# Features of the last head group weighed and decayed on VectorE, and the first set's indirect writes ended one step sooner

## The reference, cut to what matters

```
qs = softmax(q) ; ks = softmax(k)             # over the 128 features of a head
gl = log_sigmoid(k) / 16
S  = S * exp(gl) + ks x v ; o_gla = qs . S    # gated linear attention, along the tokens
y  = softmax(rot(q) rot(k)^T / sqrt(128)) v   # ordinary causal attention
o  = 0.5 * y + 0.5 * o_gla ; out = o @ Wo
```

## Time and profile before

| | before |
|---|---|
| time, median of 3 runs | 944.18 us (944.08 to 945.03) |
| profiled execution: time, span | 935.75 us, 933.5 us |
| mean granted TensorE clock | 0.994 |
| PE busy | 895.2 us (96%) |
| DVE busy | 679.4 us (73%) |
| ACT busy | 663.2 us (71%) |
| POOL busy | 635.4 us (68%) |
| chain that ended last | PE 77%, DVE 9%, ACT 5%, POOL 4%, issue 3% |

### The profile page before, as it was taken

The page is one execution under the profiler, slowest core; times in us unless marked ns, Lnnn a source line. Parts: engine busy times, 40 slices in busy tenths (PEclk is TensorE's granted clock), DMA queues, the critical chain, the costliest instruction groups (busy, mean ns, idle before and its releaser), DMA issues.

```text
span 933.5 us, 18329 instructions
## 1 busy us (share of the span) xinstructions
PE 895.2 (96%) x5145; PEld 706.8 (76%) x5145; DVE 679.4 (73%) x2010; ACT 663.2 (71%) x2147; POOL 635.4 (68%) x603
## 2 busy tenths in 40 slices
PE   7899999999999999999999999999999989799996
PEld 4577878777777777778788878787776766598885
DVE  5877877676767676767676978877888967475457
ACT  6687777777777777777686877778767767354656
POOL 6967676767566666768676767877656898546441
PEclk9999999999999999999999999999999999999999
DMA  7100100000000000620000001000003111125355
GB/s 266 35 12 29 29 24 1 6 13 7 1 0 0 0 0 7 178 62 1 1 1 2 1 1 44 1 1 17 17 17 106 40 61 41 57 86 148 109 149 202
DMA packets 30969, 41.46 MB, mean 44 GB/s; under 512 B 3230, under 2 KB 25631, under 8 KB 30624
## 3 DMA queue, kind: packets, MB, share of 16 engines
q1 hardware_dynamic: 27472, 31.98, 11.4%
q0 software_dynamic: 3408, 8.43, 2.5%
HBM read 24.72 MB, written 16.59 MB: 44 GB/s over the span
## 4 chain that ended last, share of the span: by engine, by line
PE 77%; DVE 9%; ACT 5%; POOL 4%; issue 3%; DMA 1%; DVEq 0%; POOLq 0%; ACTq 0%
PE PR L518 12%; PE OA L631 12%; PE S L585 10%; PE MS L604 8%; PE S L613 7%; PE OA L593 5%; PE OA L624 4%; PE S L731 3%; PE OA L748 3%; PE PR L564 3%; PE PR L558 3%; POOL slot_x L1717 1%; ACT eqk L879 1%; PE MS L547 1%; DVE pr L1111 1%
## 5 line engine op out<-in xcount | busy, mean ns | idle before, releaser
L1644 POOL TENSOR_TENSOR qd<-eqk,eg 128x512 f32<-128x512 f32 x63 | 75.0, 1190 | 132.3 <-issue 127.6
L631 PE MATMUL OA<-wT,V 128*128 128x512 f32 x320 | 148.4, 594 | 0.0
L841 ACT ACTIVATE S<-S,nm 128x128 f32<-128x128 f32 (+3 forms) x256 | 126.4, 494 | 6.6 <-DVE nm L1077 5.8
L1077 DVE CUSTOM_DVE_ANT_0 S<-S,maskb 128x128 f32<-128x128 f32 (+3 forms) x256 | 118.2, 518 | 13.0 <-PE S L585 11.8
L879 ACT ACTIVATE eqk<-qkv,nmx 128x128 f32<-128x128 f32 x320 | 124.3, 396 | 4.5 <-DVE nmx L1152 4.4
L1632 POOL TENSOR_TENSOR eqk<-eqk,rse 128x640 f32<-128x640 f32 x63 | 79.5, 1263 | 60.1 <-DVE rse L1195 37.0
L631 PEld LDWEIGHTS OA<-wT,V 128*128 128x128 f32 x320 | 59.8, 191 | 69.7 <-issue 69.7
L1111 DVE TENSOR_TENSOR pr<-S,rl 128x256 f32<-128x256 f32 (+3 forms) x128 | 105.5, 825 | 4.5
L1621 POOL TENSOR_TENSOR rp<-qkv,cos 128x640 f32<-128x640 f32 x64 | 99.5, 1555 | 6.8 <-ACT qkv L869 5.8
L1624 POOL TENSOR_TENSOR rp<-rp,rt 128x640 f32<-128x640 f32 x64 | 99.4, 1553 | 5.0
L1621 POOL TENSOR_TENSOR rt<-qkv,sin 128x640 f32<-128x640 f32 x64 | 99.4, 1552 | 0.0
(11 more groups left out here) (259 smaller groups left out, 2443.4 us busy)
## 6 DMA issues: line engine op xcount, KB each, us to landing
qkv<-slot_x SPq DMA_DIRECT2D x39, 129.0 KB, 2.1
slot_x<-zero SPq DMA_DIRECT2D x3, 1290.0 KB, 15.3
stage<-in_wgu SPq DMA_DIRECT2D x8, 352.0 KB, 3.1
stage<-in_wqkv SPq DMA_DIRECT2D x6, 384.0 KB, 3.7
xraw<-in_x_cols SPq DMA_DIRECT2D x16, 128.0 KB, 2.4
acc<-in_x_rows SPq DMA_DIRECT2D x1, 2048.0 KB, 11.1
dn_w<-in_wdn SPq DMA_DIRECT2D x1, 2048.0 KB, 8.2
pr<-plane SPq DMA_DIRECT2D x8, 256.0 KB, 3.9
```

Of the source, the lines that this page charges most:

```text
L631: last = pe.matmul(OA[:, :], V[:, j, :], wT[:, j, :], start=(c == 0 and j == 0), stop=(j == c))
L841: nc.scalar.activation(S[:, h, 0:n], S[:, h, 0:n], ACT.Exp, bias=nm[:, h:h + 1], scale=-1.0, accum_out=ls[:, h:h + 1]).then_inc(s_exp, 1)
L1077: nc.vector.tensor_tensor_reduce(out=S[:, h, 0:n], in0=S[:, h, 0:n], in1=maskb[:, N - n:N], scale=-1.0, scalar=FAR, op0=ALU.add, op1=ALU.m ...
```

## The change

Decay and weighing of chunks 60 to 63 (all of group 15) go from POOL to DVE. They are issued at steps 27 to 30, on DVE between the second half of the normalisation and `mask_gla`. The 24 writes of the first set stand at steps 25 to 30 with 4 in each step, where before step 30 had 6, step 31 had 2 and step 28 had none.

```
-        SEND_AT = {25: (0, 2), 26: (2, 4), 27: (4, 6), 29: (6, 8), 30: (8, 11), 31: (11, 12)}
+        SEND_AT = {25: (0, 2), 26: (2, 4), 27: (4, 6), 28: (6, 8), 29: (8, 10), 30: (10, 12)}
...
                 normalise(g, c, 1)
+                if isinstance(g, int) and C * (NG - 1) <= C * g + c + 1 < NU:
+                    decay(g, c + 1)
                 mask_gla(g, c)
...
                 later(pool, s_o, C * g + c)
-                if not (last and c == 3):
+                here = not isinstance(g, int) or C * g + c + 1 < C * (NG - 1)
+                if here:
                     weigh_features(g, c + 1)
                 move_v(g, c)
-                if not (last and c == 3):
+                if here:
                     decay(g, c + 1)
```

## The result

The changed kernel takes 947.89 us, the median of 9 runs (947.08 to 949.65), and the kernel before 944.58 us beside it (9 runs, 943.49 to 946.32). The ratio is 1.0033, with a 95% interval of 1.0023 to 1.0042: 3.3 us slower by the medians. The forecast was 944.5, and the range ended at 947.3.

The account below looks back on a forecast made before the run. PE, busy 96% of the span, was taken as the bound. Terms -6.1 - 2.4 + 3.1 + 4.8 + 0.3 + 0.65 = +0.35 gave 936.1 us profiled, and 8.43 carried over gave 944.5; range 936.3 to 947.3.

Parts of the forecast that it names:

- the clock in step 27: Step 27: PE's wait of 2.6 us was expected to cost no clock, so nothing was charged.
- rival C: Gaps in step 27 lower PE's clock: 1.7 us more, 946.2 us, up to 947.6 if step 29's slack fails; chance 0.21.
- The clock in step 29: Step 29: a slow clock after PE's 4.2 us wait, mostly absorbed by slack; term +0.3, bounds 0 and 1.7.
- PE's slack of 1.4 us: Step 29: PE's scores are ready before DVE uses them, expected to absorb about 1.4 of 1.7 us of slow clock.
- The blocking: Steps 27 and 29: DVE's decay and POOL's rotation block each other in turns; terms +3.1 and +4.8.
- The bounds: Limits on blocking: no blocking 0 in step 27, +0.4 in step 29; one wait +0.4 and +1.7.
- rival B: Partial blocking: one wait at each place gives 938.4 us, one of two places free 940 to 941.5; chance 0.15.
- rival A: No blocking in steps 27 and 29, POOL waits for DVE's five instructions: -7.45, 936.7 us; chance 0.15.
- Steps 28, 30 and 31: Step 28: decay wait gone, -2.4; step 30: later addition to `acc`, +0.65; step 31: page wait and slow clock gone, -6.1.
- it cannot be more than the wait: Step 28: the gain from removing PE's wait for the decay, -2.4, was capped at that wait's length.
- The last write: POOL's last write was expected near 791, with 6 us spare, so PE's page wait in step 31 goes.
- The level: The timed median was expected to lie 8.43 us over the profiled time, as before (944.18 against 935.75).

Follow-up runs that it names:

- after_again: The changed kernel, unedited, timed and profiled a second time: 937.95 us against 936.81 for the kernel before, ratio 1.0018.
- before_again: The kernel before, unedited, timed and profiled once more: 936.62 us against 936.51 beside it.
- decay_only: The changed kernel with the old table of writes, so only the decay moved to DVE: 937.9 us, 1.002 of the kernel before.
- sends_only: The kernel before with only the new table of writes, decay still on POOL: 932.28 us, 0.9957 of the kernel before.
- warm_gap: The changed kernel with products of zeros on PE in the gaps of steps 27 and 29: 933.79 us, 0.9972 of the kernel before.
- after_third: The changed kernel, unedited, timed and profiled a third time: 943.58 us, 0.9997 of the kernel before.
- hold_rotation: The changed kernel with POOL's rotation held until DVE's decay is through, steps 27 to 29: 928.94 us, 0.9922 of the kernel before.
- psum_operand: The changed kernel with the last group's decay on DVE reading one operand from PSUM instead of SBUF: 928.32 us, 0.9907 of the kernel before.
- after: The first measurement and profile of the changed kernel: 947.89 us against 944.58 for the kernel before, ratio 1.0033.
- hold_oldsends: The changed kernel with POOL's rotation held in steps 27 to 29 and the old table of writes: 940.71 us against 945.72, 0.9948.
- two_products: The changed kernel with DVE's last-group decay as two products instead of five instructions, weighing left out: 944.31 us, 0.9985 of the kernel before.
- hold27: The changed kernel with POOL's rotation held until DVE's decay is done in step 27 only: 940.65 us, 1.0042 of the kernel before.

## Why the prediction was wrong

**The step that failed** is the clock in step 27: "the wait is 754.8 - 752.2 = 2.6 us, nearest to the 2.38 that cost no clock, and I charge nothing." The wait was 2.34 us, even shorter, and the clock fell. It cost 1.7 us up to L585 of step 28, the price of rival C in full (1.4 in after_again). One execution had been taken for a rule: before_again has the clock falling behind the same 2.4 us in step 28, decay_only has it full behind 2.34 us in step 27. In all profiles together the clock fell behind six of the eight waits of 2.33 to 2.42 us before L564. Nor does the second, short gap of rival C decide it: decay_only has it (0.37 us) at full clock, before_again and sends_only fall without one. At this length it falls in some executions only, and a term of 0 to 1.7 with some half of it as its value was what the row allowed. warm_gap shows that the clock is a cost of its own: DVE is blocked as long, and the loss by the clock is gone.

**The clock in step 29** was sized too small, 0.3 instead of 1.1. PE's slack of 1.4 us took only a part. In after_again the term is 0.6.

**Step 29's start** came 0.4 us late in the first profile and not in after_again, so it is no part of the change.

**The blocking** in steps 27 and 29 was right, in mechanism and size: +3.1 and +4.4 (+4.9 in after_again) against +3.1 and +4.8. The bounds that it was weighed against (one wait only, or none) didn't come in those two traces, but after_third shows rival B's "one place free" in step 29. hold_rotation and psum_operand remove the blocking in two ways, and both reach what rival A was priced at: -7.6 and -8.2 us by the medians, against -7.45.

**Steps 28, 30 and 31** came as forecast (-2.6, +0.7, and -6.2 with the clock). But "it cannot be more than the wait" was wrong for step 28: where the clock falls behind that wait, as in before_again, the kernel before stands 0.9 us later at the end of the attention, and the change removes that too. The last write went at 793.86, not near 791, and 6 us to spare were more than enough. The cause was only half told: decay_only shows that the relief of POOL alone removes that wait, with PE as late as it is there.

**The level.** I carried 8.43 us over from the profiled execution to the median. That was no property of the program's work in those executions: beside the first two groups of experiments the same kernel before has its median at 936.5 to 936.8. The level cancels in the ratio. Terms of +2.7 us on 944.58 are 947.3, and 947.89 was measured.

**What stays open.** The cost of the change isn't one number: 3.3 us (1.0033), 1.1 by the medians (1.0018) and none (0.9997) in three comparisons. Two things that vary in the traces, the clock behind waits of 2.3 to 2.4 us and the meeting in step 29, are each as large as these differences; I can't show which runs had which. The one pair of profiles from executions without pauses and with the clock fallen in both, after_again and before_again, lies 1.1 us apart at the end of the attention (+2.0 and +0.9, net of the starts), as the medians of the second comparison do.

## What to carry to other kernels

Before products of two SBUF tensors move to DVE, look at what POOL runs at that moment: a row of short DVE instructions can pay a whole POOL instruction for each turn, so fuse them, keep one operand in PSUM, or hold POOL back at every place where the two can meet, not only where the trace shows it. That fusing shortens the time isn't shown here; the other two are. A wait of 2.3 to 2.4 us on PE should be charged with a good part of a clock drop. When a change has two halves, time each: here one was worth 4.5 us alone, and the other hid that.

## What the runs showed that I had not expected

- A wait of the same length is followed by the half clock in one execution and not in another: 2.38 us without it and the same wait in before_again with it; 2.34 us in step 27 with it (after) and without (decay_only).
- In some executions ACT pauses for 1 to 5 us at a time, mostly in the expert part, with nothing of the program waited for: 10.3 us in after, 12.8 in after_third, 12.0 in hold_oldsends, 5.5 in two_products (and 3.7 of DVE), none in the nine profiles whose times lie between 928 and 941 us. The last three came from one chip, where the kernel before took 945.72 us instead of 936.8. A profile of the kernel before at that level wasn't taken, so that the pauses make up this difference is likely, not shown.
- Freeing one collision made a longer one: 6.87 us for five instructions in hold27, against 1.40 at the same place in the changed kernel.
